# Full attention issued in blocks of one kind for two units, and normalisations whose scale is spread by transposes

## What is computed

```python
x = x + L0_attn(layernorm(x))   # 2 sub-layers: norm, attention of 2 heads over all 1024 keys, norm, sigmoid-gated MLP
x = x + L0_ffn(layernorm(x))    # 2 sub-layers: windowed attention of 8 heads, norm, GELU-gated MLP
x = x + L1_attn(layernorm(x))   # local attention of 16 heads merged with attention over pooled latents
x = x + L1_ffn(layernorm(x))    # 64 experts with routing by groups

# inside L0_attn, twice:
q = q / math.sqrt(DPH)
probs = jax.nn.softmax(jnp.einsum('bqhd,bkhd->bhqk', q, k), axis=-1)
att = jnp.einsum('bhqk,bkhd->bqhd', probs, v).reshape(b_, s_, h_)
```

## Time and profile before

| | |
|---|---|
| median of 3 runs | 1268.45 us (1263.98 to 1280.75) |
| the profiled execution | 1272.34 us |
| its span, first to last instruction | 1269.5 us |
| mean granted TensorE clock | 0.963 of 2.4 GHz |
| TensorE busy | 1131.2 us, 89% of the span |
| VectorE, ScalarE, GpSimd busy | 853.8, 602.7, 449.4 us |
| full attention, first score to last `mix` | 57.9 to 156.8 us, and from 240.0 us on in the second sub-layer |

### The profile page before, as it was taken

One profiled execution on the slowest core, in us unless ns is written; L12 is line 12 of the kernel. 1 busy time (PEld: TensorE's weight loads), 2 busy tenths in 40 slices (PEclk: granted clock), 3 DMA queues, 4 the chain that ended last, 5 costly groups with the idle time before them and its releaser, 6 DMA issues. The chain is left out here.

```text
span 1269.5 us, 29930 instructions
## 1 busy us (share of the span) xinstructions
PE 1131.2 (89%) x11893; PEld 726.7 (57%) x11893; DVE 853.8 (67%) x1457; ACT 602.7 (47%) x1415; POOL 449.4 (35%) x402
## 2 busy tenths in 40 slices
PE   6899999899898878989887999967898999977998
PEld 5577754577645447754445855533565354434797
DVE  3777544777545896733797843589466579988655
ACT  2665444656344668823567933310564355553000
POOL 0366500566501995510697522022444000006000
PEclk9999999999999998999998999999899899987999
DMA  3110000200001220010220000000000011100001
GB/s 75 42 43 2 1 13 17 77 2 2 2 0 34 56 57 2 3 69 1 63 62 22 3 10 19 12 3 4 3 4 4 10 24 21 18 13 1 12 26 54
DMA packets 52792, 28.10 MB, mean 22 GB/s; under 512 B 35474, under 2 KB 46268, under 8 KB 52284
## 3 DMA queue, kind: packets, MB, share of 16 engines
q1 hardware_dynamic: 52668, 26.36, 8.4%
HBM read 17.17 MB, written 1.05 MB: 14 GB/s over the span
## 5 line engine op out<-in xcount | busy, mean ns | idle before, releaser
L338 POOL TENSOR_TENSOR A_pr<-A_pr,A_rs 128x1024 f32<-128x1024 f32 x64 | 121.1, 1893 | 66.8 <-DVE A_rs L402 65.6
L392 DVE TENSOR_REDUCE A_mx<-psb 128x1 f32<-128x1024 f32 x64 | 77.8, 1216 | 21.1 <-PE psb L351 21.0
L435 ACT ACTIVATE A_pr<-psb,A_nm 128x1024 f32<-128x1024 f32 x64 | 71.4, 1115 | 22.3 <-DVE A_nm L396 22.0
L1171 POOL TENSOR_TENSOR F_raw<-F_raw,F_rc 128x1024 f32<-128x1024 f32 x32 | 75.6, 2363 | 16.6 <-DVE F_raw L1241 16.1
L362 PE MATMUL psb<-ident,A_pr 128*128 128x128 f32 x512 | 71.6, 284 | 3.1 <-POOL A_pr L338 3.1
L362 PEld LDWEIGHTS psb<-ident,A_pr 128*128 128x128 f32 x512 | 56.2, 144 | 26.0 <-POOL A_pr L338 15.2
L1986 PE MATMUL psb<-M_wd,M_gates 128*128 128x128 f32 x512 | 69.6, 279 | 0.0
L1189 PE MATMUL psb<-F_wqkv,F_hst 128*128 128x512 f32 x128 | 62.1, 609 | 6.1 <-ACT F_hst L1252 4.5
L1922 PE MATMUL psb<-XL,M_wu 128*128 128x512 f32 x128 | 67.0, 606 | 0.5 <-ACT M_ST L2046 0.5
L2229 DVE TENSOR_TENSOR M_gates<-M_hall,psb 128x512 f32<-128x512 f32 x64 | 43.9, 688 | 33.7 <-PE psb L1981 33.6
L1986 PEld LDWEIGHTS psb<-M_wd,M_gates 128*128 128x128 f32 x512 | 63.8, 191 | 4.3 <-DVE M_gates L2229 2.6
(11 more groups left out here) (369 smaller groups left out, 2927.7 us busy)
## 6 DMA issues: line engine op xcount, KB each, us to landing
F_VS<-F_V SPq DMA_DIRECT2D x62, 128.0 KB, 2.3
F_raw<-in_c_xpos_dram SPq DMA_DIRECT2D x3, 1024.0 KB, 4.9
F_wqkv<-in_L_ffn_wqkv_dram SPq DMA_DIRECT2D x3, 768.0 KB, 7.2
A_w<-in_L_attn_w_dram SPq DMA_DIRECT2D x4, 256.0 KB, 3.0
M_wu<-in_L_ffn_Wup_dram SPq DMA_DIRECT2D x16, 64.0 KB, 2.0
M_wg<-in_L_ffn_Wgate_dram SPq DMA_DIRECT2D x16, 64.0 KB, 2.1
M_wd<-in_L_ffn_Wdown_dram SPq DMA_DIRECT2D x16, 64.0 KB, 1.8
M_sel<-in_c_select_dram SPq DMA_DIRECT2D x16, 64.0 KB, 1.9
```

The costliest lines, as they stand in the source:

```text
L338: pool.tensor_tensor(p, p, rs[:, u % 2:u % 2 + 1].broadcast_to([P, SEQ]), ALU.mult).then_inc(scaled, 1)
L392: dve.tensor_reduce(mx[:, u % 2:u % 2 + 1], sview(u), AX, ALU.max).then_inc(maxed, 1)
L435: act.activation(pr[:, u % NP, :], sview(u), ACT.Exp, bias=nm[:, u % 2:u % 2 + 1], scale=scale, accum_out=su[:, u % 2:u % 2 + 1]).then_inc ...
L1171: pool.tensor_tensor(rs[:, o, :], rs[:, o, :], rc[:, o, :], ALU.add).then_inc(unit, 1)
```

## The change

Three things are altered.

First, in the full attention TensorE issues S S M T T for each tile: both scores of the next tile, `mix` of the tile before, both transposes of this tile. The transposes move through the banks by `turn_bank`: even units use 4 and 5, odd units 7 and 4, and both results of `mix` lie in bank 6, in halves (`outview`). VectorE and ScalarE follow in the same order. The second half of an odd unit's `turn` now waits for ScalarE's copy of the even unit just before it, since both use bank 4.

Second, `distribute` uses a transpose instead of a product. Third, `distribute(1)` moves out of the normalisation's own part in the merged stages, to behind the first product of the next stage, and the other two move one place down; and in n2 and n4 `finish(0)` goes ahead of the table load.

```diff
 def distribute(c):
-    last = pe.matmul(psb[:, 6 + c % 2, j * P:(j + 1) * P], rstd[:, t:t + 1].broadcast_to([P, P]), ident[:], start=True, stop=True)
+    last = pe.transpose(psb[:, 6 + c % 2, j * P:(j + 1) * P], rstd[:, t:t + 1].broadcast_to([P, P]), ident[:])
 ...
 average(3)
-distribute(1)
 if then is not None:
     then.multiply(pe, scaled if gain is None else normed, distribute)
 else:
+    distribute(1)
     distribute(2)
     distribute(3)

 # full attention
+def turn_bank(u, a2):
+    return ((4, 5), (7, 4))[u % 2][a2]
+def outview(n):
+    return psb[:, 6, n % 2 * P:(n % 2 + 1) * P]
 def turn(u):
     pe.wait_ge(scaled, u + 1)
-    for a2, kept in enumerate((kept_a, kept_v)):
-        if u:
-            pe.wait_ge(kept, u)
+    for a2 in range(2):
+        if u % 2 == 0 and a2 == 0 and u:
+            pe.wait_ge(kept_v, u)
+        if u % 2 and (a2 or u > 1):
+            pe.wait_ge(kept_a, u - 1 + a2)
 # TensorE
-for u in range(NU + 1):
-    if u + 2 < NU:
-        scores(u + 2)
-    if u:
-        turn(u - 1)
-    if u >= 3 and u % 2:
-        mix(u // 2 - 1)
+for n in range(NT):
+    if n + 1 < NT:
+        scores(2 * n + 2)
+        scores(2 * n + 3)
+    if n:
+        mix(n - 1)
+    turn(2 * n)
+    turn(2 * n + 1)
 # VectorE, behind top(0), top(1), invert(0), invert(1)
+for n in range(NT):
+    if n + 1 < NT:
+        top(2 * n + 2)
+        top(2 * n + 3)
+        invert(2 * n + 2)
+    if n:
+        put(n - 1)
+    keep(2 * n)
+    keep(2 * n + 1)
+    if n + 1 < NT:
+        invert(2 * n + 3)
 # ScalarE, behind exp(0), exp(1)
+for u in range(NU):
+    if u + 2 < NU:
+        exp(u + 2)
+    keep(u)

 # n2 (with Sigmoid) and n4 (with Gelu)
-if u in (0, 1):
-    distribute(2 + u)
+if u in (0, 1, 2):
+    distribute(1 + u)
 ...
+finish(0)
 act.activation(warm[:], eps[:, 0:1], ACT.Gelu)
-finish(0)
 # n1, between the first query and the first key product
+if n == 0:
+    distribute(1)
 # n5
-    distribute(2 + i)
+    distribute(1 + i)
+if c == 0:
+    distribute(3)
```

More of the change, by code:

```diff
@@ L356, in turn @@
                             pe.wait_ge(scaled, u + 1)
-                            for a2, kept in enumerate((kept_a, kept_v)):
-                                if u:
-                                    pe.wait_ge(kept, u)
+                            for a2 in range(2):
[3 more added lines that the diff above has]
+                                    pe.wait_ge(kept_a, u - 1 + a2)
                                 for j in range(4):
                                     k = 4 * a2 + j
-                                    last = pe.transpose(psb[:, 4 + a2, j * P:(j + 1) * P], pr[:, u % NP, k * P:(k + 1) * P], ident[:])
+                                    last = pe.transpose(psb[:, turn_bank(u, a2), j * P:(j + 1) * P], pr[:, u % NP, k * P:(k + 1) * P], ident[:])
                                 last.then_inc(turned, 1)
@@ L372, in mix @@
                                 for h in range(2):
-                                    last = pe.matmul(psb[64 * h:64 * h + 64, 6 + n % 2, 0:P], V[:, (b * TPS + k) * 2 + h, :], pt[:, n % 2, h, k, :],
+                                    last = pe.matmul(outview(n)[64 * h:64 * h + 64, :], V[:, (b * TPS + k) * 2 + h, :], pt[:, n % 2, h, k, :],
                                                      start=(k == 0), stop=(k == KB - 1), skip_group_check=True)
@@ L407, in keep @@
                                 dve.wait_ge(mixed, u // 2 - 1)
-                            dve.tensor_copy(ptile(u, 1), bank[5].rearrange("p (k n) -> p k n", n=P)).then_inc(kept_v, 1)
+                            dve.tensor_copy(ptile(u, 1), bank[turn_bank(u, 1)].rearrange("p (k n) -> p k n", n=P)).then_inc(kept_v, 1)
                         def put(n):
                             dve.wait_ge(mixed, n + 1)
-                            dve.tensor_scalar(result[:, n * P:(n + 1) * P], psb[:, 6 + n % 2, 0:P], bias, None, ALU.add).then_inc(put_out, 1)
+                            dve.tensor_scalar(result[:, n * P:(n + 1) * P], outview(n), bias, None, ALU.add).then_inc(put_out, 1)
                         top(0)
                         top(1)
[L416 to L424, removed]
+                        invert(0)
+                        invert(1)
+                        for n in range(NT):
[9 more added lines that the diff above has]
+                                invert(2 * n + 3)
                         put(NT - 1)
@@ L441, in keep @@
                                 act.wait_ge(mixed, u // 2 - 1)
-                            act.activation(ptile(u, 0), bank[4].rearrange("p (k n) -> p k n", n=P), ACT.Copy).then_inc(kept_a, 1)
+                            act.activation(ptile(u, 0), bank[turn_bank(u, 0)].rearrange("p (k n) -> p k n", n=P), ACT.Copy).then_inc(kept_a, 1)
                         exp(0)
[L445 to L449, removed]
+                        exp(1)
+                        for u in range(NU):
+                            if u + 2 < NU:
+                                exp(u + 2)
+                            keep(u)
                 clear(g)
```

## The result

The changed kernel takes 1262.79 us (median of 20 runs, 1257.09 to 1268.91), the kernel before 1270.96 (20 runs, 1263.98 to 1280.75). The ratio is 0.9938, 95% interval 0.9915 to 0.996: about 8 us, 0.6%, faster. The profiled execution took 1259.96 us, its span 1258.1 (1269.5 before), at a mean granted clock of 0.957 (0.963 before).

The account below looks back on a forecast made before the run. TensorE's own time bounds the full attention, the chain TensorE, ScalarE, VectorE the normalisations. Terms -9.4 - 4.2 - 1.8 - 1.4 + 1.8 - 1.3 + 4 = -12.3 give a median of 1256 us, range 1247 to 1268.

Parts of the forecast that it names:

- the clock term: Gaps in merged normalisations n1, n2, n4: three falls to half clock at 1.4 us each, +4 us, bounds 0 and 13.
- Blocks of one kind: Full attention, S S M T T order: fewer block edges less a new wait, 0.27 us a tile; with the ends -9.4 us.
- The first rival: Full attention: ScalarE's copy or second exponential comes 0.27 later, the 8.6 us is lost, about 1265 us; chance 0.13.
- The ends: End of each full attention: shorter waits at the last two `mix`, 0.4 us less each, 0.8 for two.
- n0, n3, n6, -4.2: Unmerged normalisations: three of four shorter spreadings lie on the chain to the last scale, 1.4 us each, -4.2.
- n1, -1.8: Merged normalisation n1, TensorE busy throughout: starts 0.44 us sooner and shorter spreadings give another 0.44; -1.8 for two.
- n5, -1.4: Normalisation n5: first product no longer behind the second spreading, VectorE's bounding work starts at 820.7 instead of 822.11; -1.4 us.
- n4, +1.8: Normalisation n4 with MLP: first product 1.95 us earlier, but two `down` waits of 1.6 return that and 0.9 more; +1.8 for two.
- n2, -1.3: Normalisation n2, built like n4 with one hidden product: fourth hidden product at 180.2 against 180.94; -1.3 us for two.
- That the spreading doesn't shorten: Rival: transpose with a repeated column takes two passes, so the spreading gains go; about 1264 us, chance 0.05.
- That the clock falls in the attention's steady part: Rival: grouped transposes bring half-clock falls in one attention tile in two, 27 us, so 1283; chance 0.05.
- The larger gain: Rival: no clock falls at all and n2, n4 less bad, -18 to -26 us, about 1247; chance 0.17.

Follow-up runs that it names:

- the run with bank 5: Changed kernel, but an odd unit's second transposing half goes to bank 5, waiting for VectorE's copy instead of ScalarE's; 1277.6 us, 1.0043 of the kernel before.
- the version with the places undone: Changed kernel with every spreading back in its old place, still by transposes, bias still ahead of the table load; 1238.96 us (0.9772), again 1245.77 us (0.9812).
- the version with products in the old places: Changed kernel with spreadings in their old places and by products again, bias still ahead of the table load; 1248.48 us, 0.9809 of the kernel before.
- the filling products: Old places, transposes, plus unread dummy products: two ahead of the next stage's first product in n1, n2, n4, three behind n0, n6's last spreading; 1236.7 us, 0.9726.

## Why the prediction was right, and where it was not

Direction and range were right: 1262.79 lies in 1247 to 1268, and within 2% of before. The centre was 6.8 too low. Of this, 2.5 is the start: 1268.45 was the median of three runs, 1270.96 that of twenty. The rest is the size: -12.3 forecast, -8.2 between the medians. Two errors partly cancel in the sum: by the stages the attention gave 2.0 more than forecast, and the normalisations with the clock term nothing where 2.9 was forecast.

- **Blocks of one kind, -9.4 forecast.** Right in mechanism, too small: -11.4 by the stages, 10 us by the run with this edit alone. The tile lost 0.32, not 0.27, so 10.2 for 32. The removed edges were as counted (S S 1.59 for 1.60, M 1.89 for 1.90); the wait, counted at 0.08, was 0.03 at most: T T took 1.93, and sixteen steps with one pair of edges are 1.90. The copy itself ran as counted, from 98.08 to 98.68, which is 1.30 after the tile's first transpose; that the weights need the bank a step earlier, at 1.27, is what didn't show. The first rival had no ground: a longer wait has its price, as the run with bank 5 shows, but here there was none. The ends gave the rest, 1.2 for 0.8. M next to S cost what I gave it, 1.89 for 1.90.
- **n0, n3, n6, -4.2.** The steps were right. Last scale of n6 before: 1022.55; the stage's start to the last scale's end went from 12.1 to 10.5, n3's stage lost 1.2. But n6 gave back twice that. Timeline of TensorE behind it, kernel after, then before:

```profile
1005.50 2.12 PE L187 MATMUL psb<-ident,n_rstd 128*128 128x128 f32 x12
1008.67 5.88 PE L1946 MATMUL psb<-M_wr,XL 128*128 128x64 f32 x32 [1.05 <-PEq L147]
...
1017.34 1.02 PE L1939 MATMUL psb<-XL,M_wu 128*128 128x512 f32 x2
```

```profile
1019.38 3.14 PE L187 MATMUL psb<-ident,n_rstd 128*128 128x128 f32 x24
1023.56 3.76 PE L1929 MATMUL psb<-M_wr,XL 128*128 128x64 f32 x32 [1.04 <-PEq L147]
...
1028.93 1.02 PE L1922 MATMUL psb<-XL,M_wu 128*128 128x512 f32 x2
```

  The spreading is 1.02 shorter, the wait the same, and then the same products take 5.88 instead of 3.76: from the block's first product to the second of L1939 8.67 against 5.37. My clock term spoke of n1, n2 and n4 only; that the unmerged norms lead into products as well was missed. How much of the stage's +2.1 is this fall is not settled: three other profiles with products and no such fall take 259.6 to 259.9 for n6, where before's took 258.3.
- **n1, -1.8.** First stage -0.6 and second -2.4, together with n0's -1.4. Less -1.4 that is -1.6. The first took the fall of the clock at 33.80 and the second lost one that it had before. The steps were right within what falls allow.
- **n5, -1.4.** VectorE's first work of the next stage starts 11.6 after the stage's start, 13.2 before: -1.6, right. These rows are of the timeline of after (compare):

```profile
807.85 1.04 PE L187 MATMUL psb<-ident,n_rstd 128*128 128x128 f32 x8
...
809.68 1.27 DVE L1497 TENSOR_SCALAR G_QM<-G_Q,G_rows 128x512 f32<-128x512 f32 x3
```

- **n4, +1.8.** The order of events came out as forecast: first product 2.4 behind the first spreading (2.5), two waits of 1.44 (1.6), fourth unit at 15.78. Of these, 1.7 are the fall over 552.60 to 556.00; without it, 14.1 as forecast. There is such a fall in the second n4 too, but the first one's stage had its 3.4 elsewhere before, so the two stages have 3.4 more at half clock (17.1 against 13.7): 1.8 + 1.7 = 3.5, against +4.3 in the stages.
- **n2, -1.3.** Wrong in sign, +0.4. By the row and the working it should have said -1.5, 0.74 for each of two. I took it that the old fall at the first hidden product goes in both. It did in the first n2, and the second has as much time at half clock as before (3.4) and pays the waits: -0.75 and +1.1. The waits, 1.44 each, are here:

```profile
168.84 1.13 PE L1088 MATMUL psb<-A_hb,A_w 128*128 128x512 f32 x2 [1.44 <-DVE A_hb L1129]
...
172.70 1.12 PE L1088 MATMUL psb<-A_hb,A_w 128*128 128x512 f32 x2 [1.44 <-DVE A_hb L1129]
```

- **The clock, +4 between 0 and 13.** The mean time at half clock went from 95 to 111. At half clock an instruction of TensorE costs double, so that is at most 7.6; over the runs of one kernel the span grows by 0.24 (with a standard error of 0.03) for each us at half clock, which makes 3.6. The term was of the right size, and so was its cause in the merged norms: I gave it to the gaps, and the table of idle times bears that out. In the profiles four of the six merged norms have a fall at their first product now, and two had one before. What it lacked is n6, whose 6.8 at half clock no term held.
- **Rivals.** That the spreading doesn't shorten: refuted, 160 entries. That the clock falls in the attention's steady part: refuted, 1.00 over 70.94 us, though T T is 1.93 in each 5.41. (The argument against it, 2.0 of transposes in any 3.4 us of the old order, holds only for T S T; from a `mix` on there are 0.6.) The larger gain, at 0.17, was there to be had, in another form: the version with the places undone is 26 us faster than before. What the prediction did not ask is what n4's new waits cost against the same edits in the old places. It compared them only with the old kernel, and a loss of some 19 us against a better neighbour looked like +1.8 in n4 and -1.3 in n2.

What stays open: the fall early in n6 came in 7 of 9 profiles with transposes there and no filling, and in none of 4 with products, though TensorE waits 1.05 for that block in both; which condition decides was not isolated. Nor is it known why at the same idle time some places have a fall and others none. The sum of the parts (attention 0.9919, transposes 0.9965, so 0.988) is 0.003 above the kernel that has just these two, 0.9852; the intervals cover it. And in n5 with the local attention, the version with products in the old places is 5.6 longer than that with transposes (203.31 against 197.71), of which 1.7 may be 3.4 more at half clock and the 3 products on the path about 1.3; I have no row for the rest.

## What to carry to other kernels

Where TensorE is full, count the edges between blocks of different shapes and order the work in few blocks, as long as the copies that free the banks come in time. Before a piece of work is moved past another on one engine, list what its consumer then does first on its own engine: here a scale put ahead of a gate made TensorE wait twice, and a table load put behind the bias paid at once. When a piece of work is made shorter and what follows still waits for another engine, the time turns into a gap, and a gap can cost more than it looks. Compare a combined change not only with the old kernel but with each part left out; a loss inside a gain is invisible otherwise.

## What the runs showed of the hardware

- **A pair of edges between blocks of different shape and array half costs 0.12 to 0.21 us on TensorE**: 0.12 for one T block more, 0.21 for an S block.
- **A gap of under 1 us ahead of a product can go with a fall of the clock to 0.50 (1.2 GHz).** Of the 84 places in the table above, none of 16 with 0.03 or less had one, 10 of 20 with 0.48, and 25 of 32 with 0.97. The row `33.80:37.20` above is one of them.
- **Whether transposes keep the clock up less than products is not settled.** The Trainium skill (TensorE: Matmul & The Clock Gate, Part 4: PE-mode transpose) says that transposes don't count as busy as products do. At the merged norms the trace doesn't show it: with 0.97 idle the falls came in 5 of 6 places with products and 20 of 26 with transposes. The mean time at half clock agrees in direction, 111 against 96 with products in the same places, and so does the start of n6, with a fall in none of 4 profiles with products and 7 of 9 with transposes. But there the transposes also left TensorE a little less busy (3.73 of the 5.00 us ahead of the block, 3.96 before), and the filling products both filled idle time and were products. And in the attention, with transposes a third of the time between full products, the clock stayed at 1.00.
- **Useless products can pay.** Two or three, of 128 columns, in a gap that was idle anyway cost nothing on the path (n1's first product comes 2.39 behind the first spreading with and without them) and brought 0.5 to 0.9%; the time at half clock went from 92 and 105 to 76.
- **A table load of 1.28 us costs its length and more** when it stands on the chain to the first product: 1.5 more of waiting at each of four places is 6, and 8 were measured (3 to 12 with the intervals), with a fall of the clock in all four.
